# Spills and later loads of the residual rows issued from ScalarE's DMA queue instead of SyncE's, in a transformer layer on eight cores

## The reference

```
x = x + attn(layernorm(x))       # lat = rmsnorm(x @ wkv_a.T); k, v = lat @ wkv_b.T
                                 # 16 heads of 128, causal softmax, then o @ out_w.T + out_b
x = x + ffn(layernorm(x))        # silu((x @ gate) * gs) * ((x @ up) * us), then (. @ down) * ds
                                 # gate, up: 2048 x 6144, down: 6144 x 2048, weights rounded to fp8
```

## Time and profile before

| | us |
|---|---|
| median of 3 runs | 1604.93 |
| lowest and highest | 1598.73, 1613.68 |
| profiled execution | 1596.11 |
| span of its slowest core (core 1) | 1594.4 |
| spans of all cores | 1589.6 to 1594.4 |

### The profile page before, as it was taken

How to read it: one execution, slowest core, us unless ns; L and a number is a source line. 1 busy time by engine, 2 the same in 40 slices (tenths; PEclk the granted TensorE clock), 3 DMA queues, 4 the chain that set the end, 5 groups by cost and what they waited for, 6 DMA issues and landing times.

```text
span 1594.4 us, 22671 instructions; the slowest of 8 cores (1589.6 to 1594.4 us)
## 1 busy us (share of the span) xinstructions
PE 1555.1 (98%) x8714; PEld 758.8 (48%) x8714; DVE 440.4 (28%) x998; ACT 363.7 (23%) x480; POOL 82.0 (5%) x174
## 2 busy tenths in 40 slices
PE   3999999999999999999999999999999999999999
PEld 2644555555555444444444444444444444444444
DVE  5735444444456661111011110111011111111111
ACT  3864565656662001101110011101110000000000
POOL 1210100000100000000000000000000000000000
PEclk9999999999999999999999999999999999999999
DMA  9953445222456995352754565372532383929210
GB/s 277 288 96 77 71 83 87 44 34 41 78 100 185 142 199 119 31 49 27 63 44 44 50 52 50 35 63 27 48 32 27 27 115 53 124 52 119 69 53 27
DMA packets 75752, 127.60 MB, mean 80 GB/s; under 512 B 46144, under 2 KB 48768, under 8 KB 70912
## 3 DMA queue, kind: packets, MB, share of 16 engines
q0 software_dynamic: 17856, 58.73, 36.6%
q1 hardware_dynamic: 57792, 67.42, 15.0%
HBM read 233.08 MB, written 16.78 MB: 157 GB/s over the span
## 4 chain that ended last, share of the span: by engine, by line
PE 91%; DMA 5%; DVE 2%; issue 1%; SPq 1%; ACT 0%; POOL 0%; DVEq 0%; ACTq 0%; POOLq 0%
PE PS L1342 21%; PE PS L1317 21%; PE PS L1323 21%; PE PS L1113 7%; PE PS L1192 4%; PE PS L1168 4%; PE PS L1122 3%; PE PS L1132 3%; PE PS L1077 3%; PE PS L1299 2%; DMA X2T<-XHb 2%; DMA WST<-wkva 1%; DMA res_scr<-RES 1%; PE PS L1141 1%; DMA X<-xq 1%
## 5 line engine op out<-in xcount | busy, mean ns | idle before, releaser
L1317 PE MATMUL PS<-X2T,W 128*128 128x512 bf16 x1536 | 347.2, 379 | 0.0
L1323 PE MATMUL PS<-X2T,W 128*128 128x512 bf16 x1536 | 347.2, 379 | 0.0
L1317 PEld LDWEIGHTS PS<-X2T,W 128*128 128x128 fp8e4 x1536 | 150.3, 98 | 181.2
L1323 PEld LDWEIGHTS PS<-X2T,W 128*128 128x128 fp8e4 x1536 | 150.3, 98 | 181.3
L880 DVE SCALAR_TENSOR_TENSOR FUSE<-PS,CF,SIL 128x512 bf16<-128x512 f32 x96 | 72.1, 751 | 587.4 <-PE PS L1323 587.4
L1032 ACT ACTIVATE SIL<-PS,CF 128x512 bf16<-128x512 f32 x96 | 66.0, 687 | 589.6 <-PE PS L1317 589.6
L957 ACT ACTIVATE P<-PS,NEGB 128x1024 bf16<-128x1024 f32 x192 | 169.9, 900 | 115.1 <-PE PS L1168 104.9
L1342 PE MATMUL PS<-WDb,FUSE 128*128 128x512 fp8e4 (+2 forms) x816 | 166.2, 366 | 0.0
L1342 PE MATMUL PS<-WDa,FUSE 128*128 128x512 fp8e4 x768 | 166.1, 379 | 0.0
L1342 PEld LDWEIGHTS PS<-WDb,FUSE 128*128 128x128 bf16 x816 | 77.9, 98 | 88.3
L1342 PEld LDWEIGHTS PS<-WDa,FUSE 128*128 128x128 bf16 x768 | 75.2, 98 | 90.6
(11 more groups left out here) (123 smaller groups left out, 946.5 us busy)
## 6 DMA issues: line engine op xcount, KB each, us to landing
W<-gu POOLq DMA_DIRECT2D x48, 512.0 KB, 9.0
WQ<-wq POOLq DMA_DIRECT2D x16, 512.0 KB, 6.7
X<-xo SPq DMA_DIRECT2D x8, 1024.0 KB, 9.1
WO<-wo POOLq DMA_DIRECT2D x16, 512.0 KB, 8.8
RES<-xq SPq DMA_DIRECT2D x8, 1024.0 KB, 7.5
res_scr<-RES SPq DMA_DIRECT2D x8, 1024.0 KB, 6.5
RB<-res_scr SPq DMA_DIRECT2D x32, 256.0 KB, 5.3
out<-OB SPq DMA_DIRECT2D x31, 256.0 KB, 2.4
```

Source lines behind the costliest of these rows:

```text
L1317: mm = e.matmul(bank(ffn_bank(f)), W8[io % 4][:, c * 128:(c + 1) * 128], X2T[:, c * 1024 + qb * 512:c * 1024 + qb * 512 + 512], start=(c = ...
L1323: mm = e.matmul(bank(ffn_bank(f) + 1), W8[io % 4][:, 2048 + c * 128:2048 + (c + 1) * 128], X2T[:, c * 1024 + qb * 512:c * 1024 + qb * 512 ...
```

## The change

SP keeps the turns only. The spill of tile t is issued by ACT, after `SD` of tile t. For t = 1 to 4 ACT then waits until the spill of tile t - 1 has landed, and issues the load of tile t + 3. The first four loads of `RES` stay on SP. Sizes, buffers and semaphores are the same.

```diff
--- before.py
+++ after.py
@@ -508,14 +508,9 @@
             e.wait_ge(d_heads[qb], 256)
         load_res(3)
         for t in range(8):
-            e.wait_ge(v_add, 4 * (t + 1))
-            e.dma_start(out=res_d.ap()[t * 128:(t + 1) * 128, :], in_=RES[t % 4][:, :]).then_inc(d_spill[t % 4], 16)
             e.wait_ge(v_xh, 16 - len(NORM_ON_ACT) + t + 1)
             e.dma_start_transpose(out=A(X2T, t * 128, [[16384, 128], [1024, 16], [1, 128]]),
                                   in_=XH2[t % 2][:, :]).then_inc(d_turn[t % 2], 16)
-            if t < 4:
-                e.wait_ge(d_spill[t % 4], 16)
-                load_res(t + 4)
         for i in range(4):
             e.wait_ge(d_spill[i], 32)
         e.wait_ge(v_xh, 24 - len(NORM_ON_ACT))
@@ -1025,6 +1020,12 @@
                     evict(job)
         for t in range(8):
             sqrt_var(16 + t)
+            e.wait_ge(v_add, 4 * (t + 1))
+            e.dma_start(out=res_d.ap()[t * 128:(t + 1) * 128, :], in_=RES[t % 4][:, :]).then_inc(d_spill[t % 4], 16)
+            if 1 <= t < 5:
+                e.wait_ge(d_spill[t - 1], 16)
+                e.dma_start(out=RES[t - 1][:, :],
+                            in_=xq_d.ap()[(t + 3) * 128:(t + 4) * 128, :]).then_inc(d_r[t - 1], 16)
         for f, (io, qb) in enumerate(FFN):
             e.wait_ge(t_g, f + 1)
             if f >= 3:
```

## The result

| | before | changed |
|---|---|---|
| median of 3 runs | 1604.93 | 1650.19 |
| ratio, 95% interval | | 1.029 [1.0233, 1.0346] |
| profiled execution, its slowest span | 1596.11, 1594.4 | 1649.12, 1647.5 |
| core executions over 1600 us | 31 of 572 | 33 of 50 |

What follows compares the result with a forecast made beforehand. The prediction took TensorE to bound the kernel (91% of the chain), with 2.5 us of waiting on core 1 in the output projection. All costs 0, gain 0.6 us: 1604.93 - 0.6 = 1604 us, range 1595 to 1613.

Steps and rivals of the forecast that it cites:

- The bound of the stage: Output projection: TensorE waits only for what DVE is late beyond 6.4 us of slack; 2.5 us on core 1.
- the transposes have SP's queue to themselves: Output projection, SP: turn 3 on core 1 lands in under 32.2 us instead of 34.6, gaining 2.5 us there.
- first sign of being wrong: SP's queue in the output projection: transposes 1 to 4 holding SP for over 18 us on average would refute the forecast.
- transposes starve beside two other queues: Output projection: transposes 1 to 4 each hold SP 28.91 us beside ACT's and POOL's transfers; 43 us, 1648; chance 0.06.
- The loads' step: Residual loads 4 to 7 in the output projection move in time but still arrive before DVE wants them; cost 0.
- ACT was right: Output projection: ACT's twelve issues, 5 us, are free and its spill waits delay no SD; the contrary rival had 0.08.
- the timed runs lose more here: Output projection: timed runs lose 2.6 to 17.6 us more than the profiled one; without it 1596 us; chance 0.14.
- The gain of 0.6 us: Whole kernel: without core 1's 2.5 us wait core 5 is slowest, so the span falls from 1594.4 to 1593.8.

Runs made afterwards that it cites:

- before_weights_early: The kernel before, with POOL's first four weight loads issued together at about 490 us, when attention has ended; ratio 0.9995.
- order_on_sync: The kernel before, all transfers still on SP, in the changed kernel's order: spill t, wait for spill t-1, load of row t+3, transpose t; ratio 1.0068, median 1612.1 us.
- take_turns: The changed kernel, with waits so that ACT's spills and loads and SP's transposes never move data at the same time; ratio 1.001.
- after_weights_late: The changed kernel, with POOL's first four weight loads issued only once all eight transposes have landed; ratio 1.0135.

## Why the prediction was wrong, point by point

**The bound of the stage was read right.** TensorE loses what DVE is late beyond 6.4 us: 59.77 - 6.4 = 53.4, measured 53.3.

**The step that failed is "the transposes have SP's queue to themselves".** It bounded a turn's landing by 4.3 and 34.6 us and took it to lie between 8.8 and 23.8 for turns 1 to 4, because "who issues doesn't make the bytes fewer". The bytes are the same (127.60 MB in both pages of the profile), but their time is not fixed: turn packets went from 0.03 to 0.48 us each in one execution, and turns 2 and 3 on core 1 landed after 85.7 and 58.8 us, with TensorE waiting 53.3 us. The bound from both sides used rows of one hardware queue for a state with two and put its upper end, 34.6 us, at the worst seen. Its own first sign of being wrong came: turns 1 to 4 hold SP for 25.7 us on average, over the 18 that it named. The prediction even said that no row of before had a second hardware queue, and then bounded it as if it had. With the worst known hold as a price, and the likelihood left open, the case would have had a much larger chance than 0.06.

**The signal was in the rows.** Core 1 had one turn of 34.6 us where the others had at most 23.8, with the same program, and the spread of the timed runs, 15 us, was called noise of the median. It was probably the same mechanism: in one measurement 11 of 142 core executions of the kernel before are over 1600, and 0 of 84 with POOL's loads ahead of the turns (before_weights_early). No core of the kernel before that was over 1600 was profiled, so this is argued and not seen. A stage that occasionally stalls for no reason that the program gives is near an edge, and the change moved it over.

**The rival "transposes starve beside two other queues" came true**, with 1648 us against 1650.19 measured. The number agrees partly by luck. It assumed four turns of 28.91 us each, deciding through turn 7 at the start of the feed-forward part; what happened is two turns of 41.16 and 51.28 us, deciding through XH2(4) in the projection. By its own formula the holds of the profiled core (1.77, 41.16, 51.28, 8.73: mean 25.7) would give 4 x (25.7 - 18.1) = 30 us, not the 43 that it put or the 51 that TensorE waited more.

**The loads' step: the cost of their dates was put at 0** and is some 0.7% (order_on_sync, 1.0068). Slack for the data was there, as computed; what the new dates change is what runs beside a turn, and that was not asked.

**ACT was right.** Twelve issues of 0.33 to 0.75 us over all cores, free; the wait for a spill never held `SD`, not even at 57 us, and not where a spill took 70.9 us to land, though the prediction had 33.7 as its limit: DVE itself was held by the turn and needed `SD` no earlier. The rule of the Trainium skill ("Perfetto Trace Analysis", section "DMA Instruction — HWDGE (DVE, Sync)") that the descriptor generator is shared and locked does not show: ACT's spill at 555.55 took 0.33 us in the midst of a turn's issue of 41.16. The Trainium skill's other page, "DMA: Bandwidth & Descriptors", section "Issuing engines are not separate DMA queues", says that the issuing engine saves issue time and nothing else; here it cost 2.9%, so the measurement decides against it for transposes in company.

**The rival "the timed runs lose more here" was probably right in its place and wrong in its remedy**: the late cores go when POOL's loads are moved (0 of 84), and not when the spills are. The median gains nothing clear of the error by it, 0.9995 and 0.999.

**The gain of 0.6 us** can't be seen in any of this.

What stays open is what happens inside the DMA engines. The runs show that ordinary transfers, POOL's converting loads and a transpose together can make the transpose's packets slow, that a turn with only one of the others beside it took 13.2 us at most (each pair seen on eight cores of a profiled execution; 16 core executions with ACT's transfers alone and 76 of take_turns have no long tail), and that it doesn't happen every time. A rate as low as the 31 in 572 of the kernel before would not show in such counts of 16. Nor is it shown what in POOL's loads matters: that they convert, that they come from a queue of another kind, or only that they are a third stream. Whether engines lose step with each other, and which order of packets starts it, no run here tells.

## What to carry to other kernels

In this kernel, splitting traffic over two queues cost 2.9% with the same bytes and nearly free issues. Beside a DMA transpose, ask first what else moves data in the same microseconds, and look at every core and every run for one that is late without a reason in the program; then try to move the third party in time, clear of the transpose, rather than transfers to another queue. A price bounded by rows of a state that the change leaves is no bound: give that case the chance that its ignorance deserves.

## What was not expected of the hardware

- Transpose packets of 256 bytes took 0.019 us beside ACT's queue alone (after_weights_late). Beside ACT's and POOL's, in the changed kernel, they took 0.030 in good moments and 0.17 and 0.48 in bad ones.
- In the bad stretch the share of DMA was 1.34 and 62 GB/s were moved; a spill took 70.9 us to land on core 1, where the shortest takes 4.1 before.
- Which core is hit changes: cores 0 and 1 took 1591.1 and 1647.5 us in one execution, and 1648.6 and 1591.3 two executions later.
